# A gated cross-attention block on one core: slot lists of DVE and ACT rearranged, part of the rest work on POOL, norm and FFN jobs in other slots, and a narrower second matmul

## The chip, the core and the metric

The kernel runs on one core of a Trainium2 chip. A core has five engines with instruction lists of their own: TensorE (PE, matrix products), VectorE (DVE), ScalarE (ACT), GpSimd (POOL) and SyncE (SP, here only DMA issues). They meet through semaphores. The metric is device time in microseconds (us); lower is better. Before the change it is 1818.12 us, the median of 3 runs (1817.14 to 1818.49).

## The reference

32 sequences of 64 tokens with 512 features, 32 heads of 128. With x the tokens and ctx the context (both 2048 x 512):

```
h   = layernorm(x)
q   = h @ Wq ; k = ctx @ Wk ; v = ctx @ Wv              (512 -> 32 heads x 128)
s   = q k^T / sqrt(128) + bias, masked keys -> -inf      (per sequence and head, 64 x 64)
a   = softmax(s) @ v
x1  = x + tanh(g_xattn) * (a @ Wo)
h1  = layernorm(x1)
out = x1 + tanh(g_ffn) * (h1 @ W^T + b + LoRA of the sequence's adapter)
```

## The kernel before

**Blocks, slots, groups.** The 2048 tokens are worked in 4 blocks of 512 (8 sequences). Each block takes the 32 heads in order, so there are 128 slots; slot n is head n % 32 of block n // 32 (s below is n % 32). Four heads make a group, whose values (v) and whose output product (o) are made together. Two sequences stand side by side on the 128 partitions, so a 128x128 score tile holds two useful 64x64 squares on its diagonal, and 4 such tiles make a block.

**Precision.** Every operand of TensorE is split in two rounded parts, `hi` (the value rounded to fp32r) and `lo` (the rest, value minus `hi`, rounded). ACT makes `hi` (L507 is its helper), then DVE (L669) or POOL (L923) makes `lo` from the source and `hi`. Large products take three matmuls of 512 columns for each of four contraction chunks, hi hi, lo hi and hi lo (`mm3`, L260 to L262). Scores and attention keep both parts of the moving operand beside each other (`kt` and `pt` have a part axis), and `both` (L264 to L266) sends all 256 columns through twice, once with the stationary `hi`, once with `lo`. The two halves of the result, in `s_two` and `pv_two`, are added later on DVE and ACT. So the product of both rests, lo lo, is formed as well.

**A slot on TensorE.** In order: q of head n (12 matmuls of 512 columns), k of head n (12), two main jobs (12 each), then in some slots one further job, then scores of head n (8 matmuls, L265 and L266 alternating) and attention of head n - 1 (8). Main jobs by n % 4: 3 and 0 have two tiles of values of the next group each, 1 and 2 two tiles each of the output product of the group before. Results of main and further jobs go to two PSUM banks in turn (`vo_bank`); a job waits on `vo_free` until the job two before it has been evacuated.

**Further jobs by s.** FFN work of the block before: statistics in slots 3 and 4 (`sums_at`), four normalise-and-turn jobs in 5 to 8 (`turn_at`), two LoRA products in 9 and 10, four dense products in 11 to 14. Leading norm of the block after: statistics in 17 and 18, turns in 19 to 22. A turn job is `normalise` on DVE (L779), four transposes on PE (L443), `hi` on ACT, `lo` on DVE. Staged pieces (`piece_at`: the dense weights for slots 5 to 8, the next context for 19 to 22, the LoRA weights in slots 5 and 6 of block 0) are rounded by ACT and their rest is taken by DVE. The x of the next block is loaded from slot 15 of SP's list.

**The softmax chain.** For head n, after PE's scores: DVE adds bias and both halves (L738) and takes the row maximum (L743), POOL subtracts it (L967, `shift`), ACT takes exp, DVE sums and inverts (L751 to L755), POOL scales (L977, `probabilities` of POOL). In slot n + 1 DVE transposes in five instructions (L713, L718; `transposes`), ACT rounds two halves of 64 rows into `pt` (L561), DVE takes the rest of the two halves (L725; `probabilities` of DVE), and PE's attention of head n, at the end of slot n + 1, waits for it (`pt_lo`).

**What sets the order.** It is written out by hand: each engine has a function `slot(n)` that lists its work, and every engine works its list strictly in that order. DVE's list before is: q rest, k rest, transposes, o weights' rest (two instructions, only where n % 4 is 3 or 0), statistics, normalise, main job 0, rest of the probabilities, main job 1, turn, LoRA, dense, piece, scores, attention sum, LoRA rest, row scales. ACT's: q, q weights, k, k weights, v or o weights, main job 0, probabilities, main job 1, turn, LoRA, piece, attention (the copy L567, then `hi` once DVE has summed), exp. POOL's: bias and mask, rests of q and k weights, rests of v weights (n % 4 is 1 or 2), deviations of a norm, shift, attention rest, scaling. SP's list loads the weights two heads ahead behind waits for the rests that free their buffers.

Of the kernel before, what the change touches and what calls it, by code (L numbers as in the profile page):

```python
# [17 lines left out]
S = 64  # L18
# [22 lines left out]

def turn_at(n):

    b, s = divmod(n, H)
    if n < SLOTS and b > 0 and 5 <= s < 9:
        return FFN, b - 1, s - 5
    if n < SLOTS and b < BLOCKS - 1 and 19 <= s < 23:
        return LEAD, b + 1, s - 19
    return None


def sums_at(n):

    b, s = divmod(n, H)
    if n < SLOTS and b > 0 and 3 <= s < 5:
        return FFN, b - 1, s - 3
    if n < SLOTS and b < BLOCKS - 1 and 17 <= s < 19:
        return LEAD, b + 1, s - 17
    return None


def lora_at(n):
    b, s = divmod(n, H)
    return (b - 1, s - 9) if n < SLOTS and b > 0 and 9 <= s < 11 else None


def dense_at(n):
    b, s = divmod(n, H)
    return (b - 1, s - 11) if n < SLOTS and b > 0 and 11 <= s < 15 else None


def piece_at(n):

    b, s = divmod(n, H)
    if n < SLOTS and b == 0 and 5 <= s < 7:
        return s - 3, "lora", s - 5
    if n < SLOTS and b > 0 and 5 <= s < 9:
        return 8 * b + s - 5, "dense", s - 5
    if n < SLOTS and b < BLOCKS - 1 and 19 <= s < 23:
        return 8 * b + 4 + s - 19, "context", s - 19  # L80
    return None
# [59 lines left out]
def flamingo_block(nc, x, ctxt, pair_bias, mask, wq, wk, wv, wo, g_xattn, g_ffn, wf, fbias, lora_a, lora_b,  # L141
                   lora_starts, lora_const, out):
    with ExitStack() as ctx:
# [9 lines left out]
        def sem(name):  # L153
# [64 lines left out]
        q_lo, k_lo, pt_lo, ot_lo, wq_lo, wk_lo, wv_lo, wo_lo, stage_lo, lead_ct_lo, lora_lo = (  # L218
            sem(f"{m}_lo") for m in ("q", "k", "pt", "ot", "wq", "wk", "wv", "wo", "stage", "lead_ct", "lora"))
# [51 lines left out]
        def _(sp):  # L271
# [65 lines left out]
            for n in range(SLOTS):  # L337
# [24 lines left out]
        def _(pe):  # L362
# [142 lines left out]
        def _(act):  # L505
# [58 lines left out]
            def attention(n):  # L564
                wait(act, ot_lo, n)
                act.wait_ge(pv_ps, n + 1)
                act.activation(by(attn, PB), pv_two[:, :, 1, :], ACT.Copy).then_inc(ot_b, 1)  # L567
                if n >= OT_BUFS:
# [90 lines left out]
            weights_vo(SLOTS)  # L659
            attention(LAST)  # L660
# [6 lines left out]
        def _(dve):  # L667
# [11 lines left out]
            def weights_o(n):  # L679
                i, g = n % G, n // G  # L680
                for k in range(2):
                    if i == G - 1:
                        dve.wait_ge(wo_hi, G * g + k + 1)
                        lo(o_w[1][:, k, :], raw_vo[k][:, :], o_w[0][:, k, :], wo_lo)
                    elif i == 0 and n > 0:
                        dve.wait_ge(wo_hi, G * (g - 1) + 2 + k + 1)
                        lo(o_w[1][:, 2 + k, :], raw_vo[k][:, :], o_w[0][:, 2 + k, :], wo_lo)
# [33 lines left out]
            def probabilities(n):  # L721
                dve.wait_ge(pt_hi, n + 1)
                for r in range(2):
                    rows = cols(r, S)
                    last = dve.tensor_tensor(pt[rows, :, 1, rows], turned[rows, :, :], f32(pt[rows, :, 0, rows]),  # L725
                                             ALU.subtract)
                last.then_inc(pt_lo, 1)
# [59 lines left out]
            def piece(n):  # L787
                z, what, c = piece_at(n)
                b = n // H
                dve.wait_ge(stage_hi, z + 1)  # L790
                if what == "lora":
                    if c == 0:
                        lo(a_w[1][:, :, :], by(stage[0], C), a_w[0][:, :, :], stage_lo)
                    else:
                        lo(b_w[1][:, :], stage[1][:, :], b_w[0][:, :], stage_lo)
                else:
                    to = ct[(b - 1) % 2] if what == "dense" else ct[(b + 1) % 2]
                    lo(to[1][:, c, :], stage[z % 2][:, :], to[0][:, c, :], stage_lo)

# [43 lines left out]
            def slot(n):  # L843
                if n > 0:
                    queries(n)
                    keys(n)
                    transposes(n - 1)
                weights_o(n)
# [4 lines left out]
                if n > 0:  # L853
                    main_job(n, 0)
                    probabilities(n - 1)
# [7 lines left out]
                if piece_at(n):  # L863
                    piece(n)
# [36 lines left out]
            probabilities(LAST)  # L901
            weights_o(SLOTS)
# [18 lines left out]
        def _(pool):  # L921
# [42 lines left out]

            def shift(n):
# [14 lines left out]
            def slot(n):  # L980
# [26 lines left out]
            for n in range(SLOTS):  # L1007
                slot(n)
            attention(LAST)
# [47 lines left out]
```

## Time and profile before

| | |
|---|---|
| median of 3 runs | 1818.12 us |
| the profiled execution's own time | 1816.8 us |
| its span, first to last instruction | 1815.0 us |
| TensorE matmul busy | 1746.3 us, 96% |
| weight loads busy (they overlap the products) | 1479.4 us, 82% |
| DVE busy | 1371.1 us, 76% |
| POOL busy | 925.1 us, 51% |
| ACT busy | 822.2 us, 45% |
| mean granted clock of TensorE | 0.988 of full |
| data moved | 168.77 MB, mean 93 GB/s |

How to read it: a matmul's duration includes the length of the array's pipeline, so matmuls overlap in the trace, and it is the distance between their starts that tells what one costs. A granted clock of 1.0 is 2.4 GHz and 0.5 is 1.2 GHz. `[0.91 <-DVE v_lo L669]` behind an instruction means that its engine sat idle 0.91 us before it, and which instruction's end let it go. PE starts slot 57 at 799.06 us, slot 58 at 811.88, slot 59 at 824.70; "+ 7.2" in the prediction means 7.2 us after PE's start of a slot.

### The profile page before, as it was taken

How to read it: one execution, taken by the hardware profiler on the slowest of the kernel's cores; microseconds unless marked ns; L12 is line 12 of the kernel's file. 1: busy time of each engine (PE TensorE's matmuls, PEld its weight loads, DVE VectorE, ACT ScalarE, POOL GpSimd, SP SyncE). 2: the span in 40 equal slices, each digit the busy share in tenths (PEclk: the TensorE clock that was granted, in tenths of full speed). 3: DMA queues.
4: the chain of work that ended last, by engine and by line, in shares of the span. 5: the costliest groups of instructions: out<-in, count | busy, mean ns of one | idle time of the engine just before them, and what ended most of it. 6: DMA issues, size and time to landing. Idle time of an engine off the chain costs nothing.

```text
span 1815.0 us, 25807 instructions
## 1 busy us (share of the span) xinstructions
PE 1746.3 (96%) x8656; PEld 1479.4 (82%) x8656; DVE 1371.1 (76%) x2897; ACT 822.2 (45%) x1608; POOL 925.1 (51%) x946
## 2 busy tenths in 40 slices
PE   5799999999999999999999999999999999999977
PEld 4688888888888888888888888888888888888856
DVE  4677778877788667887778767887778876777763
ACT  3354545444444434544444434444454543545430
POOL 3465555565654446545555534656555454545430
PEclk9899999999999999999999999999999999999988
DMA  3333233323233233333233323332323323232310
GB/s 120 91 94 105 83 121 94 116 76 105 84 100 102 93 95 97 109 95 97 90 95 100 91 93 111 92 112 86 101 84 97 93 82 99 81 100 89 86 36 24
DMA packets 93030, 168.77 MB, mean 93 GB/s; under 512 B 11313, under 2 KB 11441, under 8 KB 92898
## 3 DMA queue, kind: packets, MB, share of 16 engines
q1 hardware_dynamic: 91458, 165.52, 30.0%
q8 instruction: 70, 1.15, 0.3%
q10 hardware_dynamic: 1440, 1.59, 0.3%
q14 instruction: 62, 0.51, 0.1%
HBM read 162.88 MB, written 4.19 MB: 92 GB/s over the span
## 4 chain that ended last, share of the span: by engine, by line
PE 88%; DVE 8%; issue 2%; ACT 1%; POOL 0%; ACTq 0%; DVEq 0%
PE vo_bank L260 12%; PE vo_bank L261 12%; PE vo_bank L262 12%; PE q_bank L260 6%; PE q_bank L261 6%; PE q_bank L262 6%; PE k_bank L262 6%; PE k_bank L260 6%; PE k_bank L261 6%; PE pv_two L265 4%; PE pv_two L266 3%; PE s_two L265 3%; PE s_two L266 3%; DVE wo_lo L669 1%; DVE turned L718 1%
## 5 line engine op out<-in xcount | busy, mean ns | idle before, releaser
L967 POOL TENSOR_TENSOR score<-score,row_max 128x256 f32<-128x256 f32 x128 | 78.5, 614 | 665.5 <-DVE row_max L743 665.5
L923 POOL TENSOR_TENSOR ot_lo<-attn,ot_hi 128x512 fp32r<-128x512 f32 x128 | 165.5, 1293 | 115.2 <-ACT ot_hi L507 115.2
L567 ACT ACTIVATE attn<-pv_two 128x512 f32<-128x512 f32 x128 | 76.7, 599 | 307.0 <-PE pv_two L266 307.0
L260 PE MATMUL vo_bank<-wv_hi,ct_hi 128*128 128x512 f32 x512 | 200.1, 391 | 14.7 <-POOL wv_lo L923 14.7
L260 PE MATMUL q_bank<-xt_hi,wq_hi 128*128 128x512 f32 x512 | 203.0, 396 | 1.4 <-DVE xt_lo L669 1.4
L260 PE MATMUL vo_bank<-wo_hi,ot_hi 128*128 128x512 f32 x512 | 200.3, 391 | 3.5 <-POOL ot_lo L923 3.5
L261 PE MATMUL q_bank<-xt_lo,wq_hi 128*128 128x512 f32 x512 | 202.3, 395 | 0.0
L262 PE MATMUL q_bank<-xt_hi,wq_lo 128*128 128x512 f32 x512 | 200.5, 392 | 0.0
L261 PE MATMUL vo_bank<-wo_lo,ot_hi 128*128 128x512 f32 x512 | 200.1, 391 | 0.0
L262 PE MATMUL vo_bank<-wo_hi,ot_lo 128*128 128x512 f32 x512 | 200.0, 391 | 0.0
L261 PE MATMUL vo_bank<-wv_lo,ct_hi 128*128 128x512 f32 x512 | 199.9, 390 | 0.0
L262 PE MATMUL vo_bank<-wv_hi,ct_lo 128*128 128x512 f32 x512 | 199.9, 390 | 0.0
L262 PE MATMUL k_bank<-ct_hi,wk_lo 128*128 128x512 f32 x512 | 199.2, 389 | 0.0
L260 PE MATMUL k_bank<-ct_hi,wk_hi 128*128 128x512 f32 x512 | 199.2, 389 | 0.0
L261 PE MATMUL k_bank<-ct_lo,wk_hi 128*128 128x512 f32 x512 | 199.2, 389 | 0.0
L669 DVE TENSOR_TENSOR kt<-k_bank,kt 128x512 fp32r<-128x512 f32 x128 | 88.6, 693 | 139.5 <-ACT kt L507 139.4
L507 ACT ACTIVATE ot_hi<-attn 128x512 fp32r<-128x512 f32 x128 | 81.2, 634 | 226.0 <-DVE attn L747 226.0
L725 DVE TENSOR_TENSOR pt<-turned,pt 64x256 fp32r<-64x256 f32 x256 | 168.8, 660 | 15.7 <-ACT pt L561 14.0
L923 POOL TENSOR_TENSOR wq_lo<-raw_q,wq_hi 128x512 fp32r<-128x512 f32 x128 | 166.4, 1300 | 22.2 <-ACT wq_hi L507 22.2
L923 POOL TENSOR_TENSOR wk_lo<-raw_k,wk_hi 128x512 fp32r<-128x512 f32 x128 | 166.0, 1297 | 2.9 <-ACT wk_hi L507 2.9
L923 POOL TENSOR_TENSOR wv_lo<-raw_vo,wv_hi 128x512 fp32r<-128x512 f32 x124 | 165.4, 1357 | 0.0
L718 DVE STREAM_TRANSPOSE turned<-prob 32x128 f32<-32x128 f32 x512 | 154.9, 303 | 9.7
(107 smaller groups left out, 4246.6 us busy)
## 6 DMA issues: line engine op xcount, KB each, us to landing
raw_vo<-in_wo SPq DMA_DIRECT2D x128, 256.0 KB, 3.3
raw_q<-in_wq SPq DMA_DIRECT2D x127, 256.0 KB, 2.6
raw_k<-in_wk SPq DMA_DIRECT2D x127, 256.0 KB, 2.8
raw_vo<-in_wv SPq DMA_DIRECT2D x124, 256.0 KB, 3.3
raw_bias<-in_pair_bias SPq DMA_DIRECT2D x64, 256.0 KB, 3.2
acc<-in_x SPq DMA_DIRECT2D x16, 256.0 KB, 4.9
out<-acc SPq DMA_DIRECT2D x16, 256.0 KB, 2.0
stage<-in_ctxt SPq DMA_DIRECT2D x14, 256.0 KB, 2.6
```

The lines of the kernel that those rows point to most:

```text
L260: pe.matmul(to, left[0], right[0], start=first, stop=False)
L261: pe.matmul(to, left[0], right[1], start=False, stop=False)
L262: return pe.matmul(to, left[1], right[0], start=False, stop=last)
L265: pe.matmul(to, left[0], right, start=True, stop=False)
L266: return pe.matmul(to, left[1], right, start=False, stop=True)
L507: act.activation(to, src, func).then_inc(done, 1)
L567: act.activation(by(attn, PB), pv_two[:, :, 1, :], ACT.Copy).then_inc(ot_b, 1)
L669: dve.tensor_tensor(to, src, f32(of), ALU.subtract).then_inc(done, 1)
L718: last = dve.transpose(turned[to, :, cols(i, S // 2)], prob[of, :, cols(1 - i, S // 2)])
L725: last = dve.tensor_tensor(pt[rows, :, 1, rows], turned[rows, :, :], f32(pt[rows, :, 0, rows]), ALU.subtract)
L923: pool.tensor_tensor(to, src, f32(of), ALU.subtract).then_inc(done, 1)
L967: pool.tensor_tensor(score[:, :, :], score[:, :, :], row_max[:, :].unsqueeze(2).to_broadcast([P, PB, S]), ALU.subtract).then_inc(shift_don ...
```

## The change

1. **Narrower second matmul.** `both` sends only the `hi` part of the moving operand, 128 columns, through the stationary `lo`. The product lo lo is left out.
2. **DVE's list.** One o weight's rest and the transposes go ahead of the k rest; behind it come one half of the probabilities' rest and the second o weight's rest; then statistics, normalise, main jobs 0 and 1. The piece goes away.
3. **POOL's list.** It takes the other half of the probabilities' rest, ahead of the v weights, and the piece behind them. `pt_lo` becomes two semaphores, one for each half, and PE waits for both.
4. **ACT's list.** The v or o weights go ahead of k; probabilities and piece go ahead of the main jobs; the attention is split, so that the copy comes first, then exp, then `hi`.
5. **Slots of jobs.** They are given in lists now, and x is loaded in slot 21.

The diff, cut to its core:

```diff
+FFN_SUMS, FFN_PIECES, FFN_TURNS, LORA, DENSE = (5, 6), (7, 8, 11, 12), (9, 10, 13, 14), (15, 16), (17, 18, 19, 20)
+X_LOAD, LEAD_SUMS, LEAD_PIECES, LEAD_TURNS = 21, (22, 25), (23, 24, 27, 28), (25, 26, 29, 30)
+LORA_PIECES = (5, 6)
...
         def both(pe, to, left, right):
             pe.matmul(to, left[0], right, start=True, stop=False)
-            return pe.matmul(to, left[1], right, start=False, stop=True)
+            return pe.matmul(to[:, 0, :], left[1], right[:, 0], start=False, stop=True)
...
-                if s == 15 and b < BLOCKS - 1:
+                if s == X_LOAD and b < BLOCKS - 1:
...
-                pe.wait_ge(pt_lo, n + 1)
+                for r in range(2):
+                    pe.wait_ge(pt_lo[r], n + 1)
...
 ACT slot(n)
                 if n < LAST:
                     weights_q(n + 1)
+                weights_vo(n)
                 if n > 0:
                     keys(n)
                 if n < LAST:
                     weights_k(n + 1)
-                weights_vo(n)
+                if n > 0:
+                    probabilities(n - 1)
+                if piece_at(n):
+                    piece(n)
                 if n > 0:
                     main_job(n, 0)
-                    probabilities(n - 1)
                     main_job(n, 1)
...
-                if piece_at(n):
-                    piece(n)
+                if n > 0:
+                    attention_half(n - 1)
+                exps(n)
                 if n > 0:
                     attention(n - 1)
-                exps(n)
...
 DVE slot(n)
                 if n > 0:
                     queries(n)
+                    weights_o(n, 0)
+                    transposes(n - 1)
                     keys(n)
-                    transposes(n - 1)
-                weights_o(n)
+                    rest_of_probabilities(n - 1)
+                    weights_o(n, 1)
...
                 if n > 0:
                     main_job(n, 0)
-                    probabilities(n - 1)
                     main_job(n, 1)
...
-                if piece_at(n):
-                    piece(n)
                 scores(n)
...
 POOL
+            def rest_of_probabilities(n):
+                pool.wait_ge(pt_hi, n + 1)
+                rows = cols(0, S)
+                pool.tensor_tensor(pt[rows, :, 1, rows], turned[rows, :, :], f32(pt[rows, :, 0, rows]),
+                                   ALU.subtract).then_inc(pt_lo[0], 1)
...
 POOL slot(n)
                 if n < LAST:
                     weights_q(n + 1)
                     weights_k(n + 1)
+                if n > 0:
+                    rest_of_probabilities(n - 1)
                 weights_v(n)
+                if piece_at(n):
+                    piece(n)
                 if sums_at(n):
                     deviations(*sums_at(n))
                 shift(n)
```

DVE keeps the same subtraction for `cols(1, S)`, the lower 64 rows, and signals `pt_lo[1]`.

## Rows read from the trace of the kernel before

**Rows 1.** The page: busy us of each engine, and the granted clock in slices.

```profile
PE 1746.3 (96%) x8656; PEld 1479.4 (82%) x8656; DVE 1371.1 (76%) x2897; ACT 822.2 (45%) x1608; POOL 925.1 (51%) x946
...
PEclk9899999999999999999999999999999999999988
```

**Rows 2.** Timeline of PE in slot 57: start us, us, what.

```profile
805.21 0.39 PE L260 MATMUL vo_bank<-wo_hi,ot_hi 128*128 128x512 f32 x1
805.44 0.39 PE L261 MATMUL vo_bank<-wo_lo,ot_hi 128*128 128x512 f32 x1
...
811.64 0.28 PE L265 MATMUL pv_two<-pt,v_hi 128*128 128x256 f32 x1
811.76 0.28 PE L266 MATMUL pv_two<-pt,v_lo 128*128 128x256 f32 x1
```

**Rows 3.** Windows, columns PE, PEld, DVE, ACT, POOL busy, clock, DMA, GB/s.

```profile
811.88:824.70 12.82, 12.82 (x66) 10.93 (x65) 9.78 (x21) 5.54 (x11) 8.22 (x8) 1.00 0.37 106
255.39:349.41 94.02, 92.50 (x466) 78.08 (x465) 79.07 (x167) 47.11 (x91) 53.22 (x54) 1.00 0.32 98
490.43:573.48 83.05, 79.74 (x403) 67.13 (x402) 69.85 (x147) 42.52 (x82) 42.96 (x46) 1.00 0.32 97
...
43.17:60.18 17.01, 9.58 (x42) 7.99 (x42) 13.90 (x35) 4.30 (x9) 8.19 (x8) 0.79 0.37 100
```

**Rows 4.** Timeline of weight loads (PEld) after a wait of slot 21.

```profile
321.15 0.19 PEld L265 LDWEIGHTS pv_two<-pt,v_hi 128*128 128x128 f32 x1
321.25 0.19 PEld L266 LDWEIGHTS pv_two<-pt,v_lo 128*128 128x128 f32 x1
```

**Rows 5.** Timeline of PE around four transposes in slot 21.

```profile
319.76 0.60 PE L443 MATMUL vo_bank<-ident,xn 128*128 128x128 f32 x4
320.12 0.36 PE L265 MATMUL s_two<-kt,qt_hi 128*128 128x256 f32 x1
```

**Rows 6.** Timeline of all engines, late in slot 57.

```profile
803.76 0.61 POOL L977 TENSOR_TENSOR prob<-prob,row_scale 128x256 f32<-128x256 f32 x1
...
807.55 2.74 POOL L923 TENSOR_TENSOR wv_lo<-raw_vo,wv_hi 128x512 fp32r<-128x512 f32 x2
...
807.84 0.85 ACT L561 ACTIVATE pt<-turned 64x256 fp32r<-64x256 f32 x2 [0.90 <-DVE turned L718]
...
808.72 1.85 DVE L725 TENSOR_TENSOR pt<-turned,pt 64x256 fp32r<-64x256 f32 x2 [0.25 <-ACT pt L561]
...
810.92 0.28 PE L265 MATMUL pv_two<-pt,v_hi 128*128 128x256 f32 x1
```

**Rows 7.** Source view of line 725: min/median/max ns.

```profile
L725 DVE TENSOR_TENSOR pt<-turned,pt x256: 403/422/1564, 55.4 to 1765.9; 64x256 fp32r<-64x256 f32 x128
```

**Rows 8.** Timeline of all engines in slots 35 and 39.

```profile
500.36 1.28 DVE L766 BATCH_NORM_STATS2 stats<-acc 128x6 f32<-128x512 f32 x2
...
503.36 0.36 PE L265 MATMUL pv_two<-pt,v_hi 128*128 128x256 f32 x1 [0.91 <-DVE v_lo L669]
...
557.22 0.63 PE L443 MATMUL vo_bank<-ident,xn 128*128 128x128 f32 x4 [0.92 <-DVE v_lo L669]
```

**Rows 9.** Groups by line and form: busy us, mean ns, idle before.

```profile
L923 POOL TENSOR_TENSOR wk_lo<-raw_k,wk_hi 128x512 fp32r<-128x512 f32 x128 | 166.0, 1297 | 2.9 <-ACT wk_hi L507 2.9
...
L718 DVE STREAM_TRANSPOSE turned<-prob 32x128 f32<-32x128 f32 x512 | 154.9, 303 | 9.7
...
L967 POOL TENSOR_TENSOR score<-score,row_max 128x256 f32<-128x256 f32 x128 | 78.5, 614 | 665.5 <-DVE row_max L743 665.5
```

**Rows 10.** The page's DMA issues: count, KB each, us to landing.

```profile
raw_vo<-in_wv SPq DMA_DIRECT2D x124, 256.0 KB, 3.3
```

**Rows 11.** Timeline of PE: attention products of slots 1, 2 and the last.

```profile
58.33 0.55 PE L265 MATMUL pv_two<-pt,v_hi 128*128 128x256 f32 x1 [3.51 <-DVE pt L725]
...
73.07 0.36 PE L265 MATMUL pv_two<-pt,v_hi 128*128 128x256 f32 x1 [3.14 <-issue]
...
1766.41 0.55 PE L265 MATMUL pv_two<-pt,v_hi 128*128 128x256 f32 x1 [7.88 <-DVE pt L725]
```

More of the change, by code:

```diff
@@ L54, in sums_at @@
     b, s = divmod(n, H)
[L55 to L58, printed above, removed]
+    if n < SLOTS and b > 0 and s in FFN_SUMS:
+        return FFN, b - 1, FFN_SUMS.index(s)
+    if n < SLOTS and b < BLOCKS - 1 and s in LEAD_SUMS:
+        return LEAD, b + 1, LEAD_SUMS.index(s)
     return None
@@ L217, in flamingo_block @@
             sem(f"{m}_hi") for m in ("q", "k", "vo", "pt", "ot", "wq", "wk", "wv", "wo", "stage", "lead_ct", "lora"))
[L218 to L219 removed]
+        q_lo, k_lo, ot_lo, wq_lo, wk_lo, wv_lo, wo_lo, stage_lo, lead_ct_lo, lora_lo = (
+            sem(f"{m}_lo") for m in ("q", "k", "ot", "wq", "wk", "wv", "wo", "stage", "lead_ct", "lora"))
+        pt_lo = [sem(f"pt_lo{r}") for r in range(2)]
         vo_free, ot_b, ot_sum, acc_done = sem("vo_free"), sem("ot_b"), sem("ot_sum"), sem("acc_done")
@@ L562, in probabilities, with attention_half @@
                 last.then_inc(pt_hi, 1)
-            def attention(n):
+            def attention_half(n):
                 wait(act, ot_lo, n)
@@ L567, in attention @@
                 act.activation(by(attn, PB), pv_two[:, :, 1, :], ACT.Copy).then_inc(ot_b, 1)
+            def attention(n):
                 if n >= OT_BUFS:
@@ L677, in keys, with weights_o @@
                 lo(k_part(1), by(k_bank, PB), k_part(0), k_lo)
-            def weights_o(n):
+            def weights_o(n, k):
                 i, g = n % G, n // G
[L681 to L687, printed above, removed]
+                if i == G - 1:
+                    dve.wait_ge(wo_hi, G * g + k + 1)
+                    lo(o_w[1][:, k, :], raw_vo[k][:, :], o_w[0][:, k, :], wo_lo)
+                elif i == 0 and n > 0:
+                    dve.wait_ge(wo_hi, G * (g - 1) + 2 + k + 1)
+                    lo(o_w[1][:, 2 + k, :], raw_vo[k][:, :], o_w[0][:, 2 + k, :], wo_lo)
             def values(g, t):
@@ L719, in transposes @@
                 last.then_inc(turn_done, 1)
-            def probabilities(n):
+            def rest_of_probabilities(n):
                 dve.wait_ge(pt_hi, n + 1)
[L723 to L727, printed above, removed]
+                rows = cols(1, S)
+                dve.tensor_tensor(pt[rows, :, 1, rows], turned[rows, :, :], f32(pt[rows, :, 0, rows]),
+                                  ALU.subtract).then_inc(pt_lo[1], 1)
             def scores(n):
@@ L900, in _ @@
             transposes(LAST)
-            probabilities(LAST)
-            weights_o(SLOTS)
+            rest_of_probabilities(LAST)
+            weights_o(SLOTS, 0)
+            weights_o(SLOTS, 1)
             attention(LAST)
@@ L963, in add_bias, with piece, rest_of_probabilities @@
                 pool.tensor_tensor(at, at, mask_add[:, :, :], ALU.add).then_inc(bias_done, 1)
+            def piece(n):
+                z, what, c = piece_at(n)
+                b = n // H
+                pool.wait_ge(stage_hi, z + 1)
+                if what == "lora":
+                    if c == 0:
+                        lo(a_w[1][:, :, :], by(stage[0], C), a_w[0][:, :, :], stage_lo)
+                    else:
+                        lo(b_w[1][:, :], stage[1][:, :], b_w[0][:, :], stage_lo)
+                else:
+                    to = ct[(b - 1) % 2] if what == "dense" else ct[(b + 1) % 2]
+                    lo(to[1][:, c, :], stage[z % 2][:, :], to[0][:, c, :], stage_lo)
+            def rest_of_probabilities(n):
+                pool.wait_ge(pt_hi, n + 1)
+                rows = cols(0, S)
+                pool.tensor_tensor(pt[rows, :, 1, rows], turned[rows, :, :], f32(pt[rows, :, 0, rows]),
+                                   ALU.subtract).then_inc(pt_lo[0], 1)
             def shift(n):
```

38 lines of the change are left out of this document (14 added, 24 removed).

## Prediction, made before the changed kernel ran

> **What bounds the kernel now.** I read the page first: matmuls (PE) are busy 1746.3 us of a span of 1815.0, DVE 1371.1, and the granted clock of TensorE is at its upper level, 2.4 GHz, everywhere but in the first and the last slices [rows 1]. A high busy share says little by itself, so next come the start times of matmuls in a slot (a slot is the work of one head). Products of 512 columns start 0.23 us apart; those of 256 columns, in the score and attention products, 0.12 [rows 2]. The windows view has 12.82 for slot 58, with PE busy all through and DVE busy 9.78 of it [rows 3]. A slot has 48 products of the first kind and 16 of the second, and 48 x 0.227 + 16 x 0.120 = 12.82 us, so 0.227 is the finer value of the one spacing and nothing is left over. So in a plain slot the start spacing of matmuls is the bound, no wait is, and only spacing or count can make it shorter.
>
> The stretches with the norm jobs are different. Slots 17 to 23 of a block (statistics and turns of the next block) take 94.02 us; seven plain slots and four groups of four transposes (0.36 a group, from 319.76 to 320.12 [rows 5]) would take 91.18, so 2.8 is waiting. Slots 3 to 8 (the same for the FFN norm) take 83.05 against 78.36: 4.7 waiting [rows 3]. Three blocks have each kind: 3 x (2.8 + 4.7) = 22.5 us. The rest of the idle time is at the ends: slot 1 takes 17.01 where it holds 40 products (24 x 0.227 + 16 x 0.12 = 7.4 at full clock) [rows 3], since no main job covers its chain, slot 2 is alike, and slot 127 and what follows it wait the same way.
>
> **Part 1: the short second matmul** (`both`, 1024 products go from 256 to 128 columns). No row has a 128-column product in these number formats. Bounds: were the stream all that counts, the spacing of 256 columns less half its stream. 512 and 256 columns differ by 0.107, so 128 fewer save 0.053: spacing 0.067. From above: a spacing of 0.227, that of 512 columns, if a short stream runs at a quarter of the rate. What is nearest? Each product needs its own weight load. After a wait, with nothing in the array, two loads of the attention product start at 321.15 and 321.25 [rows 4], 0.108 apart in the trace's nanoseconds. And the transposes, which have 128 columns, start 0.109 apart: four in 0.60, less 0.27 for the last one's own length [rows 5]. So a load of 128 weights sets a floor near 0.108, which 128 columns cannot go below and which 256 already nearly touch. I take 0.112, between that floor and today's 0.120: 8 ns less each. It counts in slots 3 to 126, 124 x 8 = 992 products: 7.9 us; bounds of this reading 0 and 992 x 0.011 = 10.9.
>
> The Trainium skill (TensorE: Matmul & The Clock Gate, LDWEIGHTS) gives a weight load as its columns over 1.2, 107 ns for 128; the two loads agree. The same page (Back-to-back issue gap) has an isolated product at N/2.4 + 2.5 ns, an estimate of 56 for 128 columns: by that alone this part would give some 63 us, and the transposes at 0.109 speak against it.
>
> **Part 2: the slot lists.** In slot 57 transposes follow k's rest, ACT rounds the probabilities at 807.84 to 808.69, and DVE's two rest halves run from 808.72 to 810.57, since the second one is held up beside POOL's v weights (1.85 for two; the median of one is 0.42) [rows 6, 7]. PE wants them at 810.92: only 0.35 spare. Whatever is put before them on DVE in a slot becomes a wait of PE: the statistics (500.36, 1.28 long) stand before the main jobs and the rest halves, and PE's attention product starts at 503.36 after 0.91 idle [rows 8]; that is 1.1 to 1.2 in each of two slots of an FFN norm. The other kind is a turn: it wants the bank of main job 0, whose evacuation stands behind normalise, and starts at 557.22 after 0.92 idle [rows 8].
>
> The new DVE order, q rest, one o weight, transposes, k rest, one rest half, the other o weight, statistics, normalise, main jobs, has the transposes end at about slot + 7.2: prob is scaled at + 5.3 in slot 57 [rows 6], two tenths later as shown below, and the transposes are 4 x 0.303 [rows 9] and one more, 1.7 in all. Then come ACT's two roundings to + 8.2 and DVE's half at + 8.6 to 9.6 by whether POOL holds it up, and POOL's half, behind q's and k's weights, ends at + 9.7. POOL's half is not in the trace: its 128x256 subtractions with 256 elements a partition cost 0.61 [rows 9]; bounds 0.42 (DVE's) and 1.30 (POOL's 512-element ones [rows 9]), taken 0.65. PE wants both at + 11.8: 2.1 spare instead of 0.35, and 1.4 even at 1.30. POOL has 8.22 of 12.82 busy in slot 58 [rows 3]; 0.65 and a piece of 1.3 fit in front of `shift`, for which it idles 5 us a slot (665.5 over 128 [rows 9]). So the statistics' wait goes. K's rest ends at + 8.0; PE's scores want it at + 10.9.
>
> The turns now lie in slots with output jobs alone, without o weights and without ACT between PE and DVE: normalise ends at 9.3 to 10.3, main job 0 at 10.0 to 11.0, against a turn at + 10.9. That leaves 0.1 in most of the 24 turn slots, 2.1 in all. One of them is worse: slot 25 has the second pair of statistics and a turn, so main job 0 ends at about 12.0, 1.1 late, 3 times: 3.3. Gain of the jobs: 22.5 - 5.4 = 17.1 us (bounds 10 and 22.5). Then the next thing late in a turn slot is `scores` on DVE by 0.5, behind the turn's rest; it has 4 us spare to the next transposes.
>
> Of ACT: o/v weights go ahead of k's rounding. Their load lands 3.3 us after its issue [rows 10] and ACT asks for it at + 4.6 instead of 6.7; the issue follows POOL's v weights, at about the next slot's - 1.0, so 2 us are spare. `exps` ahead of the attention rounding moves the rounding 0.3 later and POOL's attention rest with it; output in slot 4g+1 wants it at + 5.45, it comes at 4.8. The x loads at slot 21 are 4 DMAs of SP's list behind the last store, 11 us ahead of their statistics. Semaphores, `pt_lo` as two and a second wait of PE: nothing. DVE loses 128 halves and 28 pieces; it is not the bound, so nothing.
>
> **Part 3: the ends.** In slot 1 PE waits 3.51 before the attention product at 58.33, in slot 2 3.14 at 73.07 [rows 11]. DVE's halves took 2.81 there and now one is left; the k rest comes 1.8 later, behind transposes, and PE's scores with it. Slot 1 gains 1.7, slot 2 (its k is late by PE, and transposes run before it) 2.4: 4.1. At the end the attention product of the last head, at 1766.41 after 7.88 idle [rows 11], closes a chain that loses one half (0.4), starts 1.4 earlier by the same reorder in slot 127, and has `exps` ahead of the rounding: 2.0. Bounds for both ends together: 1 and 9.
>
> **Sum.** Profiled time 1816.8, its span 1815.0 and 1.8 around it. 1815.0 - 7.9 - 17.1 - 4.1 - 2.0 = 1783.9; + 1.8 = 1785.7. The median shown is 1818.1, 1.3 above the profiled run: 1787.
>
> **Rivals.**
> (B) The waits only move. DVE's list in a turn slot is still late, each of 24 turns waits some 0.8 (were DVE's half held up 1.4 each time and normalise again): the 17.1 is gone, 1804. For it: the 1.85 of [rows 6] shows DVE held up just where its half now stands. Against: only output slots, with less on DVE.
> (C) The short product is bounded by its stream: 992 x 0.053 = 52.6 instead of 7.9: 1742. Against: both rows at 0.108.
> (D) Slower: the short product loses its rate. At 0.227 each, 992 x 0.107 = 106 more instead of 7.9 less: 1901. The decision is in one number: above 0.143 (the other parts' 23.2 us over 992 products, on top of 0.120) the change is slower than before. For it: every rounded product here has at least 256 columns. Against: transposes with 128 run at 0.109, if in another mode. The Trainium skill (FP8 and Floating Point Precision, TensorE Precision Notes) has a true fp32 product in four passes and a reduced one that truncates what it reads; four passes of 128 columns would stream as long as 512 do, and no row here shows such a product.
>
> **Chances.** Forecast 0.67, B 0.11, C 0.08, D 0.11, and 0.03 that something else, such as a DMA now late, eats the whole. The time is the likeliest one's, 1787; its own range is 1775 to 1798. The range is 1768 to 1806: it takes in the forecast and B and the bounds of spacing and ends, and leaves out C and D, 0.19. Faster by over 0.2% (3.6 us, what a measurement here can tell from none): forecast, B and C, 0.85; slower 0.12; same 0.03.
>
> **What would show it.** Spacing after a short product: 0.109 to 0.117 right, 0.067 C, 0.2 D. A plain slot of 12.76 us. Slots 3 to 8 of a block without an idle before the attention product; an idle of about 1 us before the transposes of slot 25 only. In slots 1 and 2 the wait before attention under 1 us. PE's idle near 40 us instead of 69. If DVE's half is 1.4 everywhere and turns wait, B. An attention product that waits for POOL would prove my 2.1 spare wrong.

## The result: slower, by 2.9%

The changed kernel takes 1871.13 us (median of 4 runs, 1868.49 to 1873.55), the kernel before 1817.63 (4 runs, 1816.22 to 1818.49): the ratio is 1.0295, 95% interval 1.0277 to 1.0313. I had forecast 1787. The profiled execution took 1873.55 us, its span is 1871.8.

The page of the changed kernel, first the busy times and the clock that answer to [rows 1]:

```profile
PE 1764.1 (94%) x8656; PEld 1486.2 (79%) x8656; DVE 1512.7 (81%) x2743; ACT 823.2 (44%) x1608; POOL 1085.6 (58%) x1100
...
PEclk9899999999999999999999999999999999999988
```

DVE issues 154 instructions fewer and is busy 141.6 us more. PE idles 1871.8 - 1764.1 = 107.7 us; before it was 1815.0 - 1746.3 = 68.7. The groups by form of the changed kernel, which answer to [rows 7, 9] (busy us, mean ns of one, idle before):

```profile
L765 DVE SCALAR_TENSOR_TENSOR row_scale<-row_inv,gate,row_kept 128x4 f32<-128x4 f32 x128 | 153.9, 1202 | 4.5
L682 DVE TENSOR_TENSOR wo_lo<-raw_vo,wo_hi 128x512 fp32r<-128x512 f32 x128 | 148.8, 1163 | 3.6 <-ACT wo_hi L514 1.6
L978 POOL TENSOR_TENSOR pt<-turned,pt 64x256 fp32r<-64x256 f32 x128 | 118.1, 923 | 6.3 <-ACT pt L568 6.3
L736 DVE TENSOR_TENSOR pt<-turned,pt 64x256 fp32r<-64x256 f32 x128 | 97.4, 761 | 34.5 <-ACT pt L568 34.5
L789 DVE TENSOR_SCALAR xn<-acc,mean_var,rstd 128x512 f32<-128x512 f32 x32 | 79.3, 2484 | 2.4 <-POOL rstd L945 1.7
```

and the same of the kernel before, for the three that grew:

```profile
L669 DVE TENSOR_TENSOR wo_lo<-raw_vo,wo_hi 128x512 fp32r<-128x512 f32 x128 | 90.1, 745 | 2.0
L755 DVE SCALAR_TENSOR_TENSOR row_scale<-row_inv,gate,row_kept 128x4 f32<-128x4 f32 x128 | 48.6, 380 | 4.6
L779 DVE TENSOR_SCALAR xn<-acc,mean_var,rstd 128x512 f32<-128x512 f32 x32 | 22.8, 717 | 2.1 <-POOL rstd L948 1.7
```

The same instructions on the same shapes (`wo_lo`, `row_scale`, `xn`) take 59, 105 and 57 us more. Not each of them costs the kernel time. The windows view of the changed kernel (columns as in [rows 3]; slots 29 and 30, both turn slots) shows where PE loses it:

```profile
412.76:431.19 18.43, 15.27 (x69) 12.68 (x68) 15.50 (x26) 6.01 (x12) 9.06 (x9) 0.91 0.31 97
431.19:446.11 14.92, 13.39 (x69) 11.17 (x68) 12.88 (x21) 6.29 (x13) 9.12 (x9) 1.00 0.33 90
```

Without waits a turn slot would be 12.76 + 0.36 = 13.12. I took each slot's length from PE's start of one to the next, less the products in it. A plain slot is 12.76, as forecast. Beyond that the slots 4 to 126 hold some 90 us, where before it was 22.5; about 84 of the 90 lie in the 24 turn slots, 1.8 to 5.3 in each. The slots with statistics alone have no wait any more. The timeline of all engines in slot 29 of the changed kernel (rows of the weight loads and large products left out):

```profile
422.24 0.76 DVE L736 TENSOR_TENSOR pt<-turned,pt 64x256 fp32r<-64x256 f32 x1 [0.25 <-ACT pt L568]
422.67 0.92 POOL L978 TENSOR_TENSOR pt<-turned,pt 64x256 fp32r<-64x256 f32 x1
...
423.03 3.30 DVE L789 TENSOR_SCALAR xn<-acc,mean_var,rstd 128x512 f32<-128x512 f32 x1
423.55 2.50 POOL L920 TENSOR_TENSOR wv_lo<-raw_vo,wv_hi 128x512 fp32r<-128x512 f32 x2
...
426.26 1.28 DVE L711 TENSOR_TENSOR acc<-vo_bank,acc 128x512 f32<-128x512 f32 x2
...
427.08 1.07 PE L450 MATMUL vo_bank<-ident,xn 128*128 128x128 f32 x4 [2.50 <-DVE acc L711]
...
427.80 0.56 PE L271 MATMUL s_two<-kt,qt_hi 128*128 128x256 f32 x1
...
428.27 0.52 PE L271 MATMUL s_two<-kt,qt_hi 128*128 128x256 f32 x1
```

Normalise (`xn`) takes 3.30 us where it takes 0.54 undisturbed. Its end, 426.33, lies 0.28 behind the end of POOL's two weight rests (426.05). Main job 0's evacuation stands behind it, and PE's transposes wait 2.50 for that. After the wait the products run at half the pace (two steps of `both` 0.47 apart instead of 0.23): the window's granted clock is 0.91, part of it at the lower level.

The trace of before has the same collision in 12 of its 24 turn slots, and it was cheap: `xn` took 0.67 to 1.27 us there. In the other 12, slot 39 among them, it ran undisturbed in 0.53 to 0.55. So the question is why DVE was held so much longer than in any row of before. What POOL holds up in these traces are `pt`, `wo_lo` and `row_scale`, which read two tensors from SBUF, and `xn`. The evacuations, which read one tensor from SBUF and one from PSUM, take at most 0.69 us beside POOL and without it (`kt`, `acc`).

**Reading the boundaries.** For each DVE instruction that took over 1.25 of its shortest, I looked at which of POOL's instruction ends lay in it. (The profile's spans on POOL are rough. Where two of its instructions run back to back, the second one's record starts some 0.04 us before the first one's end, in every kernel here.) In the kernel before and in that of experiment 5 below, which have no half on POOL, DVE got in at the first boundary between two such instructions: `xn` in 21 of 23 cases, `pt` in 40 of 42, the other four one instruction later. It then ends 0.28 us after the instruction that held it (`xn`, `pt`) or 0.55 (`wo_lo`). In the changed kernel DVE's `pt`, asked for during POOL's k rest, still gets in between that and POOL's half, in 121 of 121 cases. But `xn` is asked for while POOL does its half on 64 partitions, and gets in at the end of that half in 0 of 21 cases and between the two v rests in 0 of 24; only when POOL stops. `wo_lo`, asked for during the half, gets in at the boundary to the piece in 0 of 24; where POOL stops after the half, in 40 of 40.

### The profile page after: what moved, and what is told of

Its sections match the earlier page's. It is cut to its first block, busy times and chain, and to the rows that moved or that the text cites. A ratio compares the mean times of both kernels' runs of the same rounds, so it can differ in the third digit from the quotient of the medians.

```text
span 1871.8 us, 25934 instructions
## 1 busy us (share of the span) xinstructions
PE 1764.1 (94%) x8656; PEld 1486.2 (79%) x8656; DVE 1512.7 (81%) x2743; ACT 823.2 (44%) x1608; POOL 1085.6 (58%) x1100
## 4 chain that ended last, share of the span: by engine, by line
PE 61%; DVE 27%; ACT 4%; issue 4%; POOL 2%; DMA 0%; SPq 0%; ACTq 0%; DVEq 0%
PE vo_bank L266 9%; PE vo_bank L267 9%; PE vo_bank L268 9%; PE q_bank L266 5%; PE q_bank L267 4%; PE q_bank L268 4%; DVE score L748 4%; DVE wo_lo L682 4%; DVE xn L789 4%; PE k_bank L268 4%; PE k_bank L266 4%; PE k_bank L267 4%; PE pv_two L271 3%; DVE turned L730 3%; PE s_two L271 3%
## 5 line engine op out<-in xcount | busy, mean ns | idle before, releaser
L266 PE MATMUL q_bank<-xt_hi,wq_hi 128*128 128x512 f32 x512 | 213.5, 417 | 1.4 <-DVE xt_lo L682 1.4
L765 DVE SCALAR_TENSOR_TENSOR row_scale<-row_inv,gate,row_kept 128x4 f32<-128x4 f32 x128 | 153.9, 1202 | 4.5
L920 POOL TENSOR_TENSOR wv_lo<-raw_vo,wv_hi 128x512 fp32r<-128x512 f32 x124 | 156.2, 1277 | 0.0
L514 ACT ACTIVATE prob<-score 128x256 f32<-128x256 f32 x128 | 53.5, 418 | 226.5 <-POOL score L983 226.5
L682 DVE TENSOR_TENSOR wo_lo<-raw_vo,wo_hi 128x512 fp32r<-128x512 f32 x128 | 148.8, 1163 | 3.6 <-ACT wo_hi L514 1.6
```

Source lines behind the costliest of these rows:

```text
L266: pe.matmul(to, left[0], right[0], start=first, stop=False)
L682: dve.tensor_tensor(to, src, f32(of), ALU.subtract).then_inc(done, 1)
L765: dve.scalar_tensor_tensor(out=row_scale[:, :], in0=row_inv[:, :], scalar=gate[:, 0:1], in1=row_kept[:, cols(n // H, PB)], op0=ALU.mult, o ...
L920: pool.tensor_tensor(to, src, f32(of), ALU.subtract).then_inc(done, 1)
```

## The experiments

Three theories to start with. H: normalise is held by POOL, and everything behind it on DVE with it. S: the new job slots or ACT's new order cost the time. L: the lists of before would bear the new job slots as well. The ratios are to the kernel before, timed beside each of them.

**1. Normalise one slot earlier**, in DVE's list after dense and ahead of `scores`, where POOL is idle:

```diff
-                if turn_at(n):
-                    normalise(*turn_at(n))
...
+                if turn_at(n + 1):
+                    normalise(*turn_at(n + 1))
                 scores(n)
```

> The changed kernel with one thing moved: DVE's normalise of a turn is done one slot earlier, between the main jobs and the scores, when POOL has ended its list of weight rests. Theory H (held): xn takes 3.3 us instead of 0.54 in the turn slots because POOL works without a break there, and main job 0, behind it in DVE's list, makes PE wait. Then xn falls to about 0.55, the wait before the transposes (1.9 to 2.9 us) goes, and the time is near 1796 us: 1873 less 24 x 2.8 less some clock that is lost after the waits; what stays is a wait of 0.8 to 1.1 us before the output jobs of slots 9, 13, 25, 29. Rival S (slots): output slots are too full on DVE whatever xn takes; moving 0.7 us of nominal work then gives at most 24 x 0.7 = 17 us, 1855 us, and xn stays long.

Measured: 1804.58, 0.9934 (0.992 to 0.9949). `xn` is 0.54. H holds: one instruction's place is worth 66 us. I had expected 1796; 24.7 us of waits are left in slots 4 to 126, most of them before the output jobs and in slot 25.

**2. The old job slots** in the changed kernel:

```diff
-FFN_SUMS, FFN_PIECES, FFN_TURNS, LORA, DENSE = (5, 6), (7, 8, 11, 12), (9, 10, 13, 14), (15, 16), (17, 18, 19, 20)
-X_LOAD, LEAD_SUMS, LEAD_PIECES, LEAD_TURNS = 21, (22, 25), (23, 24, 27, 28), (25, 26, 29, 30)
+FFN_SUMS, FFN_PIECES, FFN_TURNS, LORA, DENSE = (3, 4), (5, 6, 7, 8), (5, 6, 7, 8), (9, 10), (11, 12, 13, 14)
+X_LOAD, LEAD_SUMS, LEAD_PIECES, LEAD_TURNS = 15, (17, 18), (19, 20, 21, 22), (19, 20, 21, 22)
```

> The changed kernel with the job slots of the kernel before (statistics 3 and 4, pieces and turns 5 to 8, LoRA 9 and 10, dense 11 to 14, x load 15, leading norm 17 to 22); all lists as changed. Half of the 24 turns are then in slots n % 4 of 3 or 0, without v weights on POOL. Theory H: xn is about 0.55 to 1.3 us in those 12 and 2.5 to 3.3 in the 12 others, so the loss is about half: about 1825 to 1835 us. Rival S: turns were cheap in these slots before, so nearly the whole loss goes: 1795 us. Rival L (lists): the loss comes with the changed lists, wherever the jobs are: stays above 1860 us.

Measured: 1879.42, 1.0351 (1.0335 to 1.0366). A miss for H's numbers, which had half the turns free and half the loss gone; the time is what L gave in this expectation, above 1860. The timeline of DVE shows why it is not better:

```profile
285.33 0.53 DVE L789 TENSOR_SCALAR xn<-acc,mean_var,rstd 128x512 f32<-128x512 f32 x1
...
314.47 4.55 DVE L789 TENSOR_SCALAR xn<-acc,mean_var,rstd 128x512 f32<-128x512 f32 x1
```

In the turn slots with no v weights `xn` is 0.53; in the 12 others POOL's run is half, two v rests and the piece, and `xn` waits for the end of all four: 4.55. The old slots are no cure, and the new ones not the cause.

**3. The narrow second product alone**, in the kernel before:

```diff
-            return pe.matmul(to, left[1], right, start=False, stop=True)
+            return pe.matmul(to[:, 0, :], left[1], right[:, 0], start=False, stop=True)
```

> The kernel before with nothing but the narrower second matmul (lo lo left out). The trace of the changed kernel has plain slots of 12.76 us instead of 12.82. If that is all that the width does: 124 x 0.06 = 7.4 us less, 1810 us. Rival: plain slots were covered by the looser lists, and with the old lists the shorter slot meets the wait for the probabilities' rest (0.35 us to spare before), so 1814 to 1818 us. Rival: less work in the array lowers the granted clock, 1820 us or more.

Measured: 1811.04 (8 runs), 0.9968 (0.9958 to 0.9979), where I expected 1810: Part 1 of the prediction holds. The kernel before took 1816.60 beside it, so the gain is 5.6. Most plain slots are 12.76 here too, but the waits of the old lists grew by some 2.5 us: the rival was right in small.

**4. POOL waits for normalise** before its v rests, in turn slots only:

```diff
             def weights_v(n):
...
+                    if turn_at(n):
+                        norm, b, t = turn_at(n)
+                        pool.wait_ge(xn_done, PB * run(norm, b) + t + 1)
```

> The changed kernel with one wait added: in turn slots POOL does not begin the rests of the v weights before DVE's xn of that slot is done. DVE's list is as changed. Theory H: xn then only meets POOL's half of the probabilities and takes 0.9 to 1.3 us instead of 3.3; main job 0 ends about 2 us earlier, and the time falls by 24 x 2 = 48 us or more, to about 1820 us or under. Rival S or any in which xn is long for a reason of its own (its operands, the DMA of x, its place in the list): xn stays at 3.3 us and POOL is only later, 1873 us or more.

Measured: 1805.14, 0.9935 (0.9921 to 0.995); `xn` 0.85. H from the other side: nothing moved on DVE, POOL only stands aside.

**5. The new job slots in the kernel before**, lists, `both` and all else as before:

```diff
+FFN_SUMS, FFN_PIECES, FFN_TURNS, LORA, DENSE = (5, 6), (7, 8, 11, 12), (9, 10, 13, 14), (15, 16), (17, 18, 19, 20)
+X_LOAD, LEAD_SUMS, LEAD_PIECES, LEAD_TURNS = 21, (22, 25), (23, 24, 27, 28), (25, 26, 29, 30)
...
-                if s == 15 and b < BLOCKS - 1:
+                if s == X_LOAD and b < BLOCKS - 1:
```

> The kernel before (its lists, its wide second matmul, pieces and both rest halves on DVE) with nothing but the new job slots. Theory H: turns now fall in n % 4 of 1 or 2, where POOL does v weights from slot + 8.5 to + 11.2 and DVE reaches xn at + 8.8; xn takes about 2.7 us instead of 0.54 to 0.9, main job 0 ends near + 12.2, and each turn waits 1.3 to 2 us: 1818 - 22 + 24 x 1.7 = about 1837 us. Rival L: the new slots are good in themselves (no o weights, no ACT step) and only the new lists spoil them: 1800 us, with xn under 1.3 us.

Measured: 1801.21, 0.9914 (0.9898 to 0.9931); waits 7.1 us. A clear miss for H as I had put it, and L was right: there, too, normalise is asked for beside POOL's v rests, but it gets in (median 0.60, source view):

```profile
L784 DVE TENSOR_SCALAR xn<-acc,mean_var,rstd x32: 512/603/1705, 18.2 to 1775.5; 128x512 f32<-128x512 f32 x32
```

The same view of the changed kernel:

```profile
L789 DVE TENSOR_SCALAR xn<-acc,mean_var,rstd x32: 517/3310/3333, 18.0 to 1847.8; 128x512 f32<-128x512 f32 x32
```

So "POOL is busy" is not enough to hold DVE for long. What differs is the kind of run that POOL makes. This sent me to the boundaries.

**6. Experiment 1 with the pieces on DVE too**:

```diff
 POOL slot(n)
-                if piece_at(n):
-                    piece(n)
...
 DVE slot(n)
                     dense(*dense_at(n))
+                if piece_at(n):
+                    piece(n)
```

> The changed kernel with the early normalise (as in the first of these runs) and the pieces' rest back on DVE behind the main jobs. In the run with early normalise alone, the second o weight of a piece slot takes 2.37 us, held beside POOL's half and the piece, and the output job of the next slot waits 1.3 to 1.5 us for the attention rest. Theory H: without the piece on POOL the o weight takes 0.7 to 1.1 us, 12 waits of about 1.3 go, and the time is about 1804.6 - 15 = 1790 us. Rival: the output job waits because exp stands ahead of the attention's rounding on ACT; then the waits stay and 26 pieces of 0.7 us on DVE bring 1804 to 1808 us.

Measured: 1798.64, 0.9897 (0.9883 to 0.9912). `wo_lo` is at most 1.12 now, 5.9 us are won. Some 18.5 us stay. PE idles 0.74 before the transposes of each slot 25, and 0.45 to 0.73 before each of 12 output jobs that wait for POOL's `ot_lo`:

```profile
PE vo_bank L266 <- POOL ot_lo L935: 9.3, 13, 3.5
```

(waits of PE: us in total, times, longest; the thirteenth, 3.5 us, is at the kernel's end).

**7. The changed kernel with the pieces on DVE**: the diff of experiment 6 on it, without experiment 1's.

> The changed kernel with only the pieces' rest back on DVE; normalise stays where the change has it. Theory H: xn stays at 3.3 us (POOL's half and the v weights still run there), only the waits before the output jobs of slots 9, 13, 25, 29 shrink: about 1871 - 12 = 1859 us. Rival: the pieces on POOL are the main cause: under 1830 us.

Measured: 1865.65, 1.0265 (1.025 to 1.028). `xn` is 3.3 as in the changed kernel; the pieces cost 5.5 us, not the bulk.

**8. Experiment 6 with ACT's attention ahead of exp again**, in one block as before:

```diff
                 if n > 0:
                     attention_half(n - 1)
-                exps(n)
-                if n > 0:
                     attention(n - 1)
+                exps(n)
```

> As the run with early normalise and pieces on DVE, and ACT's end of a slot as before the change (copy, rounding of the attention, then exp). Theory H says that row_scale is 1.2 us instead of 0.38 because POOL's attention rest now overlaps it, and that it is off PE's path in plain slots; with the order back it is 0.4, and the time is the same as of that run or up to 6 us less, where a late chain made an output job wait. Rival: exp first is what keeps the plain slot at 12.76 with the shorter matmuls; then plain slots grow and the time is 1800 us or more.

Measured: 1790.73, 0.9854 (0.984 to 0.9869): 7.9 us better. In both orders `row_scale` (four columns) meets POOL's attention rest `ot_lo`, and ends 0.02 us after it. With exp first it is asked for 0.10 us after that rest's start and takes 1.21; with exp last, 0.93 after it, and takes 0.38. The wait of the output jobs falls from some 0.46 to 0.14.

**9. Both halves of the rest on DVE**, as before, in the changed order:

```diff
 POOL slot(n)
-                if n > 0:
-                    rest_of_probabilities(n - 1)
...
 DVE rest_of_probabilities(n)
-                rows = cols(1, S)
+                for r in range(2):
+                    rows = cols(r, S)
```

> The changed kernel with POOL's half of the probabilities' rest back on DVE; everything else as changed. So far: xn got in at a boundary between two of POOL's instructions in every case but two in the kernels with the old lists (27 of 29), and at none of the 24 first boundaries in the changed one, where its request comes during POOL's half, which works on 64 partitions. Theory Q (POOL's half shuts the run): without it xn gets in at the next boundary, xn is 0.6 to 1.5 us, no xn is 3.3, and the time falls by 24 x 1 to 2: 1820 to 1845 us. Rival G (one grant after another is refused): DVE's first half gets in, then the second half and xn wait until POOL stops; the sum of the two is 3 us or more, and the time stays at 1865 to 1875 us.

Measured: 1864.59, 1.0257 (1.0241 to 1.0272). Q's time is missed by 20 us and G's is nearly met, but not for G's reason. The time looks as if nothing had happened, yet it is another loss. All 124 requests of `pt` that met a boundary between two of POOL's instructions got in at the first one, 62 of them between the two v rests:

```profile
424.48 2.18 DVE L737 TENSOR_TENSOR pt<-turned,pt 64x256 fp32r<-64x256 f32 x2 [0.25 <-ACT pt L568]
426.70 1.38 DVE L790 TENSOR_SCALAR xn<-acc,mean_var,rstd 128x512 f32<-128x512 f32 x1
```

`xn` falls from 3.30 to 1.38, so it was POOL's half that shut the boundaries. Yet each of three DVE instructions in a row now waits for the end of another POOL instruction. `xn` ends no earlier than at + 11.4, the 24 turn slots still lose some 66 us, and six slots without a turn are 13.24 or 13.28 instead of 12.76. Moving half of the rest to POOL was thus right in itself, once POOL's half no longer holds DVE (experiment 12).

**10. POOL's half over all 128 partitions**, same columns, same DVE list:

```diff
                 rows = cols(0, S)
-                pool.tensor_tensor(pt[rows, :, 1, rows], turned[rows, :, :], f32(pt[rows, :, 0, rows]),
+                pool.tensor_tensor(pt[:, :, 1, rows], turned[:, :, :], f32(pt[:, :, 0, rows]),
```

> The changed kernel with POOL's half done over all 128 partitions instead of 64 (same 256 elements in each, so about the same time; the quarter that should stay zero gets the unrounded values, so attention's second part is not the reference's). Theory Q1: it is the 64-partition form that keeps DVE out for the rest of POOL's run; then xn and the second o weight get in at the next boundary, xn is about 0.85 to 1.3 us, and the time is 1820 to 1835 us. Rival Q2: it is the place of the instruction or its two readers, or the grant given to DVE just before, not the partitions: xn stays at 3.3 us and the time at 1871 us.

Measured: 1790.52, 0.9855 (0.984 to 0.987), better than the best I had expected. (This kernel writes unrounded values into the quarter of `pt` that must stay zero, so it serves for its time alone.) The slot-29 timeline:

```profile
415.95 0.93 POOL L978 TENSOR_TENSOR pt<-turned,pt 128x256 fp32r<-128x256 f32 x1
416.31 0.85 DVE L789 TENSOR_SCALAR xn<-acc,mean_var,rstd 128x512 f32<-128x512 f32 x1
416.83 2.72 POOL L920 TENSOR_TENSOR wv_lo<-raw_vo,wv_hi 128x512 fp32r<-128x512 f32 x2
```

POOL's instruction is as long (925 ns on 128 partitions, 923 on 64), the order is the same, and `xn` gets in at the half's end, 416.88, and is through at 417.16: in 21 of 21 cases, `wo_lo` in 24 of 24. So the hold comes with the instruction that leaves half of the partitions out, not with its time or place. Nor is it a matter of a gap: the v rests start 0.05 before the half's end here, and `xn` gets in.

**11. The new slots and the narrow product**, the diffs of experiments 5 and 3 together in the kernel before.

> The kernel before with the new job slots and the narrower second matmul, its lists untouched. The new slots alone were 1801.2 us and the narrow matmul alone 1811.0 against 1816.8. If the two add: 1801.2 - 5.8 = 1795.4 us. Rival: shorter slots meet the old lists' late rest of the probabilities and eat it: 1799 us or more.

Measured: 1797.17, 0.9887 (0.9873 to 0.9902), against a sum of 1795.4: the two parts all but add, 20.7 us without touching a list.

**12. POOL waits for the end of its own half.** Is it the 64 partitions as such (P), or that POOL's next instruction starts on the idle partitions before the half is complete (C)? A wait tells them apart:

```diff
                 if n > 0:
                     rest_of_probabilities(n - 1)
+                    pool.wait_ge(pt_lo[0], n)
                 weights_v(n)
```

> The changed kernel with one wait added: POOL goes on to the v weights or the piece only when its own half of the probabilities' rest has ended; the half keeps its 64 partitions. Theory C (carry-over): the half's idle partitions let the next instruction begin under it, so that POOL's run has no boundary until it stops; with the wait the boundary behind the half is there again, xn and the second o weight get in at it (0.85 and about 1.1 us), and the time is 1788 to 1796 us. Rival P: a 64-partition instruction on POOL shuts DVE out by itself whatever follows when; then xn stays at 3 us or more and the time at 1866 us or more.

Measured: 1789.97, 0.9852 (0.9836 to 0.9869). C holds, P falls. The timeline of slot 29:

```profile
412.29 0.92 POOL L978 TENSOR_TENSOR pt<-turned,pt 64x256 fp32r<-64x256 f32 x1
...
412.65 0.85 DVE L789 TENSOR_SCALAR xn<-acc,mean_var,rstd 128x512 f32<-128x512 f32 x1
...
413.29 2.61 POOL L920 TENSOR_TENSOR wv_lo<-raw_vo,wv_hi 128x512 fp32r<-128x512 f32 x2
...
414.40 0.60 PE L450 MATMUL vo_bank<-ident,xn 128*128 128x128 f32 x4
```

POOL's v rests start 0.08 after the half's end (413.21); in the changed kernel they started 0.04 before it (423.55 against 423.59), as back-to-back instructions do everywhere. With the wait `xn` ends at 413.50 and PE's transposes wait for nothing. The page of this kernel:

```profile
PE 1734.3 (97%) x8656; PEld 1467.9 (82%) x8656; DVE 1429.2 (80%) x2743; ACT 825.0 (46%) x1608; POOL 1100.7 (62%) x1100
```

Against the changed kernel the span is 1871.8 - 1788.6 = 83.2 shorter. Of these 53.4 are less idle time of PE (107.7 to 54.3), and 29.8 are less busy time for the same products (1764.1 to 1734.3). Of the 29.8, 25.9 lie in slots 4 to 126, where the granted clock had fallen behind many of the waits (0.99 on the mean there, 1.00 now). Another 3.6 lie ahead of slot 4, where the code is the same and the clock was 0.94 instead of 0.86 in this execution.

**13. The best of all**: experiment 8 with three moves.

```diff
-X_LOAD, LEAD_SUMS, LEAD_PIECES, LEAD_TURNS = 21, (22, 25), (23, 24, 27, 28), (25, 26, 29, 30)
+X_LOAD, LEAD_SUMS, LEAD_PIECES, LEAD_TURNS = 21, (22, 23), (23, 24, 27, 28), (25, 26, 29, 30)
...
 DVE slot(n)
                     main_job(n, 0)
+                if piece_at(n):
+                    piece(n)
+                if n > 0:
                     main_job(n, 1)
...
-                if piece_at(n):
-                    piece(n)
-                if turn_at(n + 1):
-                    normalise(*turn_at(n + 1))
                 scores(n)
                 if n > 0:
                     attention(n - 1)
+                if turn_at(n + 1):
+                    normalise(*turn_at(n + 1))
```

> The run with early normalise, pieces on DVE and ACT's old order (1790.7 us) with three more moves: normalise behind the attention sum, where DVE waits 1.06 us for exp and POOL has just ended shift; the piece between the main jobs, where DVE waits for v; and the leading norm's second statistics in slot 23 instead of 25. Of the 11.6 us that its slots 4 to 126 lose, slot 25 has 3 x 1.4 and the output jobs of slots 9, 13, 25, 29 about 0.5 each. Theory H: both go, and the time is 1781 to 1784 us with xn at 0.54. Rival: xn in that place holds up the sum and row scale, the attention rest comes later, and the time is 1790 us or more.

Measured: 1784.26 (1782.86 to 1785.46), 0.9817 (0.9801 to 0.9834), the fastest here; 3.6 us of waits are left in slots 4 to 126, and `xn` has its bare length:

```profile
L789 DVE TENSOR_SCALAR xn<-acc,mean_var,rstd x32: 516/539/548, 18.1 to 1757.0; 128x512 f32<-128x512 f32 x32
```

## Why the prediction was wrong

**The step that failed** is one phrase of Part 2: "normalise ends at 9.3 to 10.3". It ended at + 11.9 to 13.9. I read the price of a blocked DVE instruction from [rows 6, 7] as a property of DVE's instruction (1.4, though [rows 7] has 1.56 as the longest), and used POOL's new work only as time on POOL ("0.65 and a piece of 1.3 fit"). The forecast was a gain of 17.1 in Part 2. It became a loss of some 67.5 (waits of 22.5 to 90). With `xn` at 3.30 in 21 turn slots and 1.83 in the 3 slots 25, main job 0 is evacuated at + 12.5 to 14.5, where I had 10.0 to 11.0 (12.0 in slot 25). Rival B had the right place (turn slots, DVE held) but 0.8 a turn; it was 3.5. My range left out any hold longer than a row of before showed, although the change put a new kind of instruction into the very run of POOL that does the holding. There lay the missing bound: a hold to the end of POOL's run, 0.65 + 2.7 by [rows 6], some 3.3 us. 24 of these, less the 1 us or so that a turn has spare, make about 55: a rival of 1840 or so that I could have priced. (The chances of forecast, B and C add to 0.86, not 0.85.)

**The mechanism.** Of DVE's `xn`, `pt`, `wo_lo` and `row_scale` in the changed kernel, 405 were asked for while a POOL instruction ran, and 404 ended only behind its end (the other one ran beside a small `rstd`). They get in at a boundary between two of POOL's instructions, and POOL pays in turn: the piece behind the half takes 1.74 us in experiment 10, where `wo_lo` gets in ahead of it, and 1.28 in the changed kernel. Behind an instruction that uses only half of the partitions the boundary does not appear, nor do the next ones in the run, until POOL has wholly stopped or has waited for completion. Shown: the hold goes with the 64 partitions (experiment 10) and with the missing wait (12). The Trainium skill (GPSIMD Engine Reference, Instruction dispatch) says that a POOL core serves its own 16 partitions and "starts instruction N+1 as soon as it finishes its share of N"; four of the eight cores have no share in the half, so they would be an instruction ahead for the rest of the run, and POOL would never be between instructions. Experiments 10 and 12 agree, but no trace shows the cores singly, so this reading is argued. The skill (SBUF — State Buffer, SBUF: two separate sides) has the port pair held "for the whole instruction"; the runs show that for adjacent instructions it can be held for the whole run, 3.3 and 4.55 us. Whether POOL's half on partitions 64 to 127 would do the same stays open: no run has a time for it.

**Part 1** was right: a plain slot of 12.76, 0.06 less, 7.4 in 123 slots where I had 7.9, and 5.6 when made alone. The starts after a short product (two steps of `both` are 0.23 apart) rule out rivals C and D.

**The other points of Part 2.** The idle before the attention product in the slots with statistics is gone, as forecast. PE waits for POOL's `pt` only twice, at the ends, so the 2.1 spare was there. POOL's half is 0.92, not 0.65, within my bounds and without effect. "Then the next thing late" was not `scores` but `ot_lo` for output jobs: I had it at 4.8 against 5.45, and in slot 29 it was 0.65 late. `exps` goes first, `row_scale` is 1.2 beside `ot_lo`, and the whole chain shifts: 7.9 us in the kernel of experiment 8, not measured in the changed one. And `wo_lo` is held to 2.35 in piece slots; 5.5 us (experiment 7).

**Part 3** was about right. Ahead of slot 4 PE idles 3.9 less (27.7 us instead of 31.6; forecast 4.1), but slot 4 starts only 2.6 earlier, since the products took 1.3 longer; other runs with the same code in the first slots start it 2.5 to 6.8 earlier, by how the clock rises there. Slot 127 and what follows is 1.2 shorter (2.0 forecast). The wait before the attention product of slot 1 is gone; it now stands before the scores, 5.84 instead of 3.92.

**What the plan was worth without the hold**: experiment 12 leaves the whole change in place and adds one wait. Its 1789.97 is 3 us from my 1787. The turn slots wait 5.9 us in all where I had 5.4 (1.3 in slot 25 where I had 1.1, about 0.1 in most others). So the sum for the turns was sound, and its assumption on DVE beside POOL was not. That the total comes so near is in part luck. The LoRA and dense slots wait 5.0 us, for which I had nothing, and against that slot 4 starts 6.2 earlier in its profiled execution where I had 4.1, with the clock at 0.94 there instead of 0.90 before. PE's idle time, which I had near 40, is 54.3.

## What to carry to other kernels

Before moving work to POOL, ask what DVE will ask for while POOL runs, and price each such request at the end of POOL's whole run of adjacent instructions, not of one. A POOL instruction on half of the partitions, as tried here, should have a wait for its own completion behind it, or cover all partitions where the data allow it, if DVE needs SBUF soon after. And place DVE instructions that POOL can hold and that stand on a chain where POOL idles: one such move gave 66 us here.

## What was not expected of the hardware

- One wait of POOL for itself decides some 80 us. It costs a gap of 0.08 us behind the half and lets DVE in, 21 of 21 times; without it a 0.54 us instruction takes 3.3. Behind a half done over all 128 partitions DVE gets in 21 of 21 times with no gap at all.
- A four-column DVE instruction (`row_scale`, 0.22 us the one time it ran free) takes 1.2 beside POOL's 512-element subtraction, 127 times.
- POOL's subtraction with a rounded result costs 923 ns on 64 partitions and 925 on 128 (256 elements a partition): leaving half of the partitions out saves nothing. Its unrounded one of the same size, `score`, costs 614 [rows 9].
- Behind PE's waits of 1.5 to 2.5 us its granted clock often fell to the lower level for a while, in the same slot or the next (0.91 in slot 29, but 1.00 in slot 61 after waits as long, and 0.93 in slot 62). The slower products were 25.9 us of the 83.2 by which the span shrank.
